# Last batch of attention: who masks three units of first-pass scores, the banks of the output blocks, and the place of one wait

## The reference, cut to what matters

```python
scores = jnp.einsum('bhqd,bhkd->bhqk', qh, kh) * inv_sqrt_d
scores = jnp.where(causal, scores, jnp.finfo(scores.dtype).min)
attn = jax.nn.softmax(scores, axis=-1)
out = jnp.einsum('bhqk,bhkd->bhqd', attn, vh)
...
x = x + attention(layernorm(x))
logits = (h @ router_w.T + router_b).reshape(T, O, E)
w, sel = top_k(softmax(logits), 2)          # per token and output element
expert_out = einsum('th,eoh->teo', h, expert_w) + expert_b
x = x + sum of the two chosen expert_out, weighted by w / sum(w)
```

## Time and profile before

| | us |
|---|---|
| median of 3 runs | 1962.87 |
| lowest and highest | 1961.36, 1963.85 |
| profiled execution, its own time | 1961.69 |
| its span in the profile | 1960.0 |
| TensorE busy | 1906.1 (97%) |
| VectorE busy | 1430.7 (73%) |
| ScalarE busy | 1042.6 (53%) |
| GpSimd busy | 842.8 (43%) |

### The profile page before, as it was taken

The page is one execution under the profiler, slowest core; times in us unless marked ns, Lnnn a source line. Parts: engine busy times, 40 slices in busy tenths (PEclk is TensorE's granted clock), DMA queues, the critical chain, the costliest instruction groups (busy, mean ns, idle before and its releaser), DMA issues.

```text
span 1960.0 us, 30381 instructions
## 1 busy us (share of the span) xinstructions
PE 1906.1 (97%) x9772; PEld 1512.2 (77%) x9772; DVE 1430.7 (73%) x2840; ACT 1042.6 (53%) x2064; POOL 842.8 (43%) x1016
## 2 busy tenths in 40 slices
PE   4899999999999999999999999999999999999999
PEld 3667777777766788888888888888888888888887
DVE  5677677777657847978798888587777777777752
ACT  2575665666554438777778777643333344333330
POOL 5587777777674133654554453111111231111110
PEclk8999999999999999999999999999999999999999
DMA  6454554555467377868864555922222232222211
GB/s 168 112 124 129 153 134 128 137 145 131 112 164 273 134 262 229 273 225 250 266 217 167 213 192 192 337 81 89 93 80 81 91 113 97 81 91 92 81 43 33
DMA packets 103838, 294.56 MB, mean 150 GB/s; under 512 B 13793, under 2 KB 14817, under 8 KB 98626
## 3 DMA queue, kind: packets, MB, share of 16 engines
q1 hardware_dynamic: 91538, 209.44, 33.6%
q10 hardware_dynamic: 8880, 67.37, 10.5%
q0 software_dynamic: 3328, 16.78, 3.7%
HBM read 150.31 MB, written 109.16 MB: 132 GB/s over the span
## 4 chain that ended last, share of the span: by engine, by line
PE 91%; DVE 4%; ACT 2%; issue 1%; DMA 1%; SPq 0%; ACTq 0%; POOL 0%; DVEq 0%; POOLq 0%
PE pair L268 22%; PE pair L270 22%; PE pair L269 22%; PE pair L681 4%; PE ps L730 4%; PE pair L714 4%; PE ps L268 3%; PE ps L269 3%; PE ps L270 3%; PE ps L750 1%; DVE nmax L1410 1%; DVE pair L1416 1%; ACT pT L1108 1%; PE ps L913 1%; PE pair L687 1%
## 5 line engine op out<-in xcount | busy, mean ns | idle before, releaser
L268 PE MATMUL pair<-w_h,hT 128*128 128x512 f32 x1920 | 750.4, 391 | 1.5 <-issue 1.4
L270 PE MATMUL pair<-w_h,hT 128*128 128x512 f32 x1920 | 747.4, 389 | 0.0
L269 PE MATMUL pair<-w_l,hT 128*128 128x512 f32 x1920 | 747.2, 389 | 0.0
L1931 POOL TENSOR_TENSOR logits<-logits,second 128x512 f32<-128x512 f32 x224 | 298.6, 1372 | 592.8 <-DVE second L1628 592.5
L268 PEld LDWEIGHTS pair<-w_h,hT 128*128 128x128 f32 x1920 | 360.4, 188 | 76.9 <-issue 2.9
L270 PEld LDWEIGHTS pair<-w_h,hT 128*128 128x128 f32 x1920 | 360.4, 188 | 75.5
L269 PEld LDWEIGHTS pair<-w_l,hT 128*128 128x128 f32 x1920 | 360.5, 188 | 73.7
L1731 DVE SCALAR_TENSOR_TENSOR xb<-pair,c_all,xb 128x512 f32<-128x512 f32 x256 | 191.8, 749 | 179.7 <-PE pair L270 174.8
L1108 ACT ACTIVATE pT<-pair,zero 128x1024 f32<-128x1024 f32 (+3 forms) x256 | 202.7, 792 | 199.9 <-PE pair L714 187.2
L1416 DVE CUSTOM_DVE_ANT_0 pair<-pair,future 128x256 f32<-128x256 f32 (+3 forms) x340 | 184.4, 555 | 120.7 <-PE pair L681 114.4
L1213 ACT ACTIVATE w<-tree 128x512 f32<-128x512 f32 x32 | 20.2, 632 | 387.3 <-DVE tree L1630 387.3
(11 more groups left out here) (165 smaller groups left out, 2605.1 us busy)
## 6 DMA issues: line engine op xcount, KB each, us to landing
logits<-lg_all ACTq DMA_DIRECT2D x32, 1792.0 KB, 8.6
qk_st<-qk SPq DMA_DIRECT2D x372, 128.0 KB, 2.5
lg_all<-ev_a SPq DMA_DIRECT2D x30, 768.0 KB, 8.8
lg_all<-ev_b SPq DMA_DIRECT2D x29, 768.0 KB, 3.8
xb<-x SPq DMA_DIRECT2D x64, 256.0 KB, 4.1
hT_all<-hT SPq DMA_DIRECT2D x32, 512.0 KB, 4.4
hT<-hT_all SPq DMA_DIRECT2D x32, 512.0 KB, 3.9
xt<-in_x SPq DMA_DIRECT2D x8, 1024.0 KB, 5.6
```

What stands on the lines that cost most here:

```text
L268: pe.matmul(dst, lh, rh, start=start, stop=False)
L269: pe.matmul(dst, lh, rl, start=False, stop=False)
L270: return pe.matmul(dst, ll, rh, start=False, stop=stop)
L1931: pool.tensor_tensor(logits[t % 2][:, e - 1, :], logits[t % 2][:, e - 1, :], second[:], ALU.subtract)\
```

## The change

`masked` gets a third argument. Its condition is `v in (3, 4) or (c == 0 and v > 4 and not last)`, by the precedence of `and`: the narrow units stay as they were in all batches, and in the last batch the three steps (0, 5), (0, 6) and (0, 7) are computed head by head and masked by VectorE. `out_bank` puts the output blocks that are projected in the last batch in the two task banks in turn; the other batches keep bank 0. And VectorE's wait for the stores of all sums moves from in front of `fix_rest` to behind it.

```diff
--- before.py
+++ after.py
@@ -274,9 +274,13 @@
             k = v + LEAD
             return 1 + k // UNITS, k % UNITS
 
-        def masked(c, v):
-
-            return v in (3, 4) or c == 0 and v > 4
+        def masked(c, v, last):
+
+            return v in (3, 4) or c == 0 and v > 4 and not last
+
+        def out_bank(i, last):
+
+            return i % 2 if last else 0
 
         def block_of(v):
 
@@ -832,8 +836,8 @@
                             pe.wait_ge(s["o_hi"], (b - 1) * KC + chunk + 1)
                             pe.wait_ge(s["o_lo"], (b - 1) * KC + chunk + 1)
                         if chunk == 0:
-                            take(0, "WO", (b - 1) * QB + i)
-                        project_out(b - 1, i, chunk, 0)
+                            take(out_bank(i, last), "WO", (b - 1) * QB + i)
+                        project_out(b - 1, i, chunk, out_bank(i, last))
 
                     def turn_tokens(i):
                         take(1 - i % 2, "LNT", (b + 1) * QB + i)
@@ -844,7 +848,7 @@
                         final = last and c == KC - 1
                         shifted_scores(n, c, v, final)
                         g, vv = target(c, v - 1)
-                        if not masked((c if v else c - 1) % KC, (v - 1) % UNITS) and (more or c + g < KC):
+                        if not masked((c if v else c - 1) % KC, (v - 1) % UNITS, last) and (more or c + g < KC):
                             scores(n + g, (c + g) % KC, vv, (1,))
                         if c == 0 and v in VALUE:
                             take(0, "V", b * QB + VALUE[v])
@@ -871,7 +875,7 @@
                             project(v)
                         g, vv = target(c, v)
                         if more or c + g < KC:
-                            if masked(c, v):
+                            if masked(c, v, last):
                                 scores(n + g, (c + g) % KC, vv, mask=True)
                             else:
                                 scores(n + g, (c + g) % KC, vv, (0,))
@@ -1492,7 +1496,7 @@
                                 scaled(n - 1, (c - 1) % KC)
                         i = None if first else summed_block(c, v, last)
                         if i is not None:
-                            residual(b - 1, i, 0)
+                            residual(b - 1, i, out_bank(i, last))
                         if (c, v) == key_rest(c) and ahead:
                             lo_of(n + AHEAD, KL, "k", key_bank(c))
                         if c == 0 and more:
@@ -1503,7 +1507,7 @@
                             block_statistics(b + 2, STATISTICS.index((c, v)))
                         g, vv = target(c, v)
                         if more or c + g < KC:
-                            maxima(n + g, (c + g) % KC, vv, masked(c, v))
+                            maxima(n + g, (c + g) % KC, vv, masked(c, v, last))
                         if QUERY.get(v) == KC - 1 and ahead:
                             lo_of(n + AHEAD, QL, "q", 1)
                         if last:
@@ -1591,12 +1595,6 @@
             for b in range(B):
                 body(b, b == 0, b < B - 1, b < B - 2)
             epilogue()
-
-
-
-
-            for k in range(2):
-                dve.wait_ge(s[f"x1_out{k}"], B * QB // 2 * 16)
 
             def best_two(t, piece):
 
@@ -1712,6 +1710,8 @@
                 for piece in pieces[3:]:
                     post(*piece)
             fix_rest()
+            for k in range(2):
+                dve.wait_ge(s[f"x1_out{k}"], B * QB // 2 * 16)
             for t in range(FIRST, NT):
                 route(t, t % 2)
```

## The result

The changed kernel takes 1964.23 us (median of 22 runs), the kernel before on the same chip 1961.36 us (22 runs): ratio 1.0015, 95% interval 1.0009 to 1.0021. The forecast was 1960.8 us in a range of 1957.8 to 1962.6. The profiled execution after took 1963.78 us with a span of 1962.0, 2.0 us over the span of the profile before; the medians lie 2.9 us apart. Lines of the kernel after are 4 higher than before in the attention part: L714 is now L718, L1410 is L1414, L1416 is L1420, L1000 is L1004, L385 is L389.

The account below looks back on a forecast made before the run. TensorE, busy 97% of the span, was taken as the bound. Gains of 1.4 + 0.75 + 1.15 = 3.3 us less 2.4 us for the low clock, 0.9 net, took 1961.69 to 1960.8 us; range 1957.8 to 1962.6.

Parts of the forecast that it names:

- part A: Last batch's three wide units masked by VectorE: TensorE starts c = 1 earlier, saving 1.4 us, bounds 0 and 3.6.
- Rival (4): Shift rows for c = 1 land still later, after 6.3 us at 574.3: slower, 1964.0 us; chance 0.05.
- The price of the new idleness: A low clock moves behind TensorE's 2.9 us wait for the rows, after 572.3: 2.4 us lost, between 0 and 3.4.
- Part B: Two output banks remove residual waits: 0.46 us at block 1, 0.29 at block 3; 0.75 us saved, bounds 0 and 1.5.
- Part C: Moved wait for stores removes VectorE's 1.67 us idleness and TensorE's pause near 641: 1.15 us saved, bounds 0.5 and 1.2.
- its other reading: At c = 1, the second shift row really waits for the 1 MB load's end near 571.7; 572.3 taken as landing.
- rival (3): Waits for the maxima, 1.3 + 0.2 us, still bring the low clock at 567, 0.7 us lost: 1959.1 us; chance 0.14.

Follow-up runs that it names:

- e1: The changed kernel with ScalarE's second 1 MB router load at step (1, 0) instead of (0, 7); ratio to the kernel before 0.9988.
- e3: The kernel before with only its first two router loads one step earlier, at (0, 5) and (0, 6); ratio to before 1.0022.
- e10: The changed kernel with its first three router loads at (1, 0), (2, 0) and (2, 2); ratio to before 0.9976, 1955.94 us beside 1960.32.
- e15: The kernel before plus two banks, the moved wait and router loads at (1, 0), (2, 0), (2, 2), masks still on TensorE; ratio to before 0.9985.
- e4: The changed kernel with banks and wait set back, so only the masks on VectorE remain; ratio to before 1.0028.
- e2: The changed kernel with its first two router loads at (1, 0) and (1, 1) instead of (0, 6) and (0, 7); ratio to before 1.0009.
- e9: The changed kernel with its first two router loads at (1, 0) and (1, 2) instead of (0, 6) and (0, 7); ratio to before 0.9995.
- e5: The kernel before with only the last batch's output blocks in two banks in turn; ratio to before 1.0000.
- e6: The kernel before with only VectorE's wait for the stores moved behind the repairs; ratio to before 0.9995.
- e12: The kernel before with only VectorE's masks and the second router load at (1, 0) instead of (0, 7); ratio to before 1.0003.
- e13: The kernel before with two banks and the moved wait, masks still on TensorE and router loads in their old places; ratio to before 0.9988.
- e7: The kernel before with only its first two router loads moved to (1, 0) and (1, 2); ratio to before 1.0001.
- e11: The changed kernel with its six router loads at (1, 0), (2, 0), (3, 0), (3, 1), (3, 2) and (3, 3); ratio to before 0.9987.
- e14: The kernel before with only its first three router loads moved to (1, 0), (2, 0) and (2, 2); ratio to before 0.9998.

## Why the prediction was wrong

**The failed step** is the one in part A that reads "The load stays where it is. So the row lands at 567.72 + 0.3 + 4.5 = 572.5". It is nearly right for the first router load (565.39 before, 564.89 after) and overlooks the second. ScalarE's second load is issued behind the exponential of step (0, 7), and this is the exponential that the masks, and the missing low clock, bring forward. It went from 568.95, behind the row, to 567.11, ahead of it. The row then took 8.3 us and landed at 576.0. Instead of 1.4 us won, part A lost 2.5 us at this place. e1 and e3 show it from both sides: take the load away and the wait falls to 1.4 us, bring it forward in the kernel before and a wait of 3.3 us is there. Rival (4) named the way it would go, a later landing, but priced it at 6.3 us of landing and gave it 0.05, since nothing in the working made the landing later; with 8.3 us its own sum gives 1961.69 + 2.5 + 3.4 - 1.9 = 1965.7 us. Its 1964.0 us lie near the 1964.23 measured by luck: the landing is put too early and the low clock too dear.

**The price of the new idleness** was mis-sized: 2.4 us forecast, 1.5 us read from two executions (18.60 against 17.12 us). That it would come was right. In e10 and e15, where TensorE idles 1.4 and 1.7 us in one piece and nowhere longer between 560 and 600 us, it didn't come there.

**Part A's own gain** was too high as well. 1.4 us were counted against a profile in which the low clock stood; with no load ahead of the row on either side VectorE's masks save 0.72 us (e10 against e15). And such a profile was the rarer kind: of the 114 executions of before beside the experiments 17 show a mean granted clock of 0.993, as the profiled one does, and take 1962.4 us in the mean; 50 show 0.995 and take 1959.8. All 22 of the changed kernel show 0.992 or 0.993. If the 22 executions of before in the main comparison were like these (their clocks are not on record), the change puts a low clock where there mostly was none. The order, the 1.37 us of idleness and the start of the value matmuls were right to 0.1 us.

**Part B** was right in its mechanism: 0.77 us become 0.4 for the maxima (forecast 0.3), 0.4 us won at block 1 (forecast 0.46). At block 3 the 0.29 us didn't show as such: the way from c = 2 to c = 3 took 16.75 instead of 16.86 us, with 0.56 us of waiting for the next row in it instead of 0.29.

**Part C** was right in its mechanism and short in its size: 1.5 us (19.11 to 17.60) instead of 1.15. At the place itself the lag falls from 3.04 to 1.93 us, that is 1.1; the rest lies mainly at the second group, which starts 2.85 us behind the first instead of 3.13.

The sum by these sizes: +2.5 for the row, +1.5 for the low clock, -0.4 -0.1 for the banks, -1.5 for the wait make +2.0 us, the difference of the two spans. Between the medians it is 2.9 us; the low clock of before, which most of its executions seem to lack, would make up for such a difference, but no trace of a typical one was taken.

The Trainium skill ("DMA: Bandwidth & Descriptors", section "Anatomy of one DMA — SWDGE (gpsimd) path") has a fixed cost of about 2.0 us for a DMA that GpSimd issues. The rows are issued by SyncE, so it is only a near case, here as in the prediction: e10 agrees with 1.9 us with no load in flight, the change with 8.3 us doesn't. The Trainium skill's section "Queues, rings and completion order" on the same page has each DMA engine take turns between the queues that it has work for. The runs agree in part: with two loads ahead of it the row landed before the second of them (576.04 against 578.05 us in the change, 573.12 against 575.05 in e3, 574.42 against 577.04 in e4). But at c = 1 no row issued behind a load that was in flight got by with 1.9 us; the shortest took 3.0 us (the high row of e1).

## What to carry to other kernels

When an engine gets faster, list every DMA that is issued behind it, and set its new time against the small transfers that the critical engine waits for: here 1.8 us earlier put 1 MB ahead of 8 KB and cost 2.5 us. Bulk loads that are not needed for 40 us belong behind the small copy of their stage, one at a time; each other gap in this kernel had a transfer of SyncE's to hit, the copies in e2 and the store in e9. What is hit need not be the transfer that the engine waits for: in e9 it was a store, two transfers ahead of the row in SyncE's program. And a wait that the profile doesn't show may be hidden by a low clock: before counting a gain there, look for what is late next in an execution without it.

## What the runs showed of the hardware that was not expected

A transfer of 8 KB on SyncE's queue is held up by transfers of 1 MB on ScalarE's. The second row of c = 1 takes 1.9 us with none ahead of it, 3.3 to 4.5 us with one (before, e1, e5, e6, e12, e13) and 6.2, 7.4 and 8.3 us with two (e3, e4, the change). With one it lands 0.4 to 0.7 us behind that load's end in all six, which tells more than its own duration does; the prediction had this as its other reading ("the end of the load near 571.7"). It is not the only thing that slows such a row: at c = 3 it took 2.9 to 3.7 us in twelve of the sixteen kernels and 1.9 in four (e3, e7, e9, e11), with no router load in flight in any of them, and why stays open.

And the low clock doesn't follow a wait of a given length: in the profile of before it lies at 567 us, behind 1.71 us of idleness, and in that of e6, whose order up to there is the same, none lies behind the same 1.71 us, and the same way takes 7.70 us against 9.36. With TensorE's masks the wait for the maxima is 1.7 us in all eight profiles, and within 2 us behind it the granted clock falls to 0.50 in three (before, e7, e14); e3's falls later, in the wait for the row. With VectorE's masks that wait is 1.4 us, and in none of the eight profiles does the clock fall right behind it, so rival (3) of the prediction didn't come up. What decides stays open.
